# Expert batches of 4, 5 and 7 groups in units of 128 rows, and combining placed by a count of gathers, in a graph and mixture-of-experts kernel

## The reference, cut to what matters

```python
# x: (8192, 128), adj: (8192, 8192), 16 experts, 2 chosen for each row
msg = layernorm(x) @ W + B
weights = where(adj < 1, exp(-(1/adj - 1)**2 / 0.5), 0)
x = x + weights @ msg
z = layernorm(x)
logits = z @ gate_w + gate_b
vals, idx = top_k(logits, 2)
share = softmax(vals)
h = relu(z @ w1[e] + b1[e])                       # for each chosen expert e, 256 wide
moe = sum over the two of share * (h @ w2[e] + b2[e])
x = x + layernorm(z + moe) * gamma + beta
```

## Time and profile before

| | us |
|---|---|
| median of 3 runs | 1823.88 (1822.68 to 1824.42) |
| the profiled execution's span, first to last instruction | 1823.2 |
| PE busy | 1624.7 (89%) |
| ACT busy | 1565.7 (86%) |
| DVE busy | 1499.7 (82%) |
| POOL busy | 463.6 (25%) |
| chain of waits that ended last: PE L1118, PE L1137 | 48%, 24% of the span |
| mean granted clock of TensorE | 0.951 of 2.4 GHz |

### The profile page before, as it was taken

The page is one execution under the profiler, slowest core; times in us unless marked ns, Lnnn a source line. Parts: engine busy times, 40 slices in busy tenths (PEclk is TensorE's granted clock), DMA queues, the critical chain, the costliest instruction groups (busy, mean ns, idle before and its releaser), DMA issues.

```text
span 1823.2 us, 24195 instructions
## 1 busy us (share of the span) xinstructions
PE 1624.7 (89%) x8178; PEld 1073.6 (59%) x8178; DVE 1499.7 (82%) x2298; ACT 1565.7 (86%) x1502; POOL 463.6 (25%) x342
## 2 busy tenths in 40 slices
PE   4999999999999999999999999999999987384720
PEld 3666666666666666666666656666666786373620
DVE  7999998989899999999999989999998443153464
ACT  5899999999999999999999999999999664253531
POOL 0001223131314040407132231313140213535342
PEclk9999999999999999999999999999999999696765
DMA  9559867676767676776776676787673244343431
GB/s 313 158 160 290 235 199 215 195 217 193 214 195 212 196 212 198 220 213 202 210 202 209 199 210 199 209 247 208 202 206 121 80 124 143 87 141 97 129 110 50
DMA packets 216792, 338.22 MB, mean 186 GB/s; under 512 B 18080, under 2 KB 74144, under 8 KB 216544
## 3 DMA queue, kind: packets, MB, share of 16 engines
q1 hardware_dynamic: 208368, 319.62, 59.8%
q0 software_dynamic: 8304, 17.06, 3.1%
HBM read 303.07 MB, written 33.55 MB: 185 GB/s over the span
## 4 chain that ended last, share of the span: by engine, by line
PE 84%; DVE 6%; another core or an unknown queue 5%; issue 3%; ACT 1%; DMA 1%; DVEq 0%; SPq 0%; ACTq 0%
PE acc L1118 48%; PE tp L1137 24%; PE tp L1164 4%; PE tp L1192 3%; PE acc L1192 2%; DVE chunk L654 1%; PE tp L1153 1%; DVE stats L666 1%; DVE chunk L660 1%; DVE chunk L1004 1%; PE misc L1094 1%; ACT chunk L613 1%; DVE msg L729 1%; DMA xs<-in_x_dram 1%
## 5 line engine op out<-in xcount | busy, mean ns | idle before, releaser
L1118 PE MATMUL acc<-wT,msg 128*128 128x512 f32 x2048 | 976.0, 599 | 0.0
L527 ACT ACTIVATE wT<-tp 128x1024 f32<-128x1024 f32 x512 | 761.0, 1674 | 14.0 <-PE tp L1137 12.4
L521 ACT ACTIVATE chunk<-chunk 128x2048 f32<-128x2048 f32 x256 | 655.3, 2560 | 0.1
L660 DVE SCALAR_TENSOR_TENSOR chunk<-chunk 128x2048 f32<-128x2048 f32 x256 | 584.8, 2284 | 54.7 <-ACT chunk L521 54.1
L1137 PEld LDWEIGHTS tp<-ident,chunk 128*128 128x128 f32 x4096 | 478.7, 141 | 223.2 <-issue 221.5
L654 DVE SCALAR_TENSOR_TENSOR chunk<-chunk 128x2048 f32<-128x2048 f32 x256 | 583.5, 2280 | 1.9 <-DMA chunk<-in_adj_dram 1.9
L1137 PE MATMUL tp<-ident,chunk 128*128 128x128 f32 x4096 | 534.3, 274 | 0.0
L516 ACT ACTIVATE chunk<-chunk 128x4096 f32<-128x4096 f32 x118 | 511.0, 4331 | 0.0
L1118 PEld LDWEIGHTS acc<-wT,msg 128*128 128x128 f32 x2048 | 349.1, 190 | 258.3 <-issue 245.8
L457 POOL TENSOR_TENSOR pool_carrier<-pool_carrier 1x1 f32<-1x1 f32 x32 | 43.7, 1365 | 951.5 <-DVE row_now L845 825.9
L476 POOL DMA_INDIRECT rows_in<-y,row_now x128 | 216.7, 1693 | 40.4 <-issue 40.4
(11 more groups left out here) (121 smaller groups left out, 794.7 us busy)
## 6 DMA issues: line engine op xcount, KB each, us to landing
chunk<-in_adj_dram SPq DMA_DIRECT2D x256, 1024.0 KB, 5.4
chunk<-rows_in SPq DMA_DIRECT2D x118, 64.0 KB
rows_out<-chunk SPq DMA_DIRECT2D x59, 128.0 KB
chunk<-rows_in SPq DMA_DIRECT2D x35, 128.0 KB
rows_out<-chunk SPq DMA_DIRECT2D x17, 256.0 KB
y_kept<-y SPq DMA_DIRECT2D x16, 256.0 KB, 6.1
chunk<-y_kept SPq DMA_DIRECT2D x16, 256.0 KB
out_dram<-chunk SPq DMA_DIRECT2D x16, 256.0 KB
```

The lines of the kernel that those rows point to most:

```text
L521: act.activation(slot(c), slot(c), ACT.Exp, scale=-1.0).then_inc(inverted, 1)
L527: act.activation(wT[:, (g * PPG + m) % WSLOTS, :], tp[(g * PPG + m) % TSLOTS][:, :], ACT.Exp, scale=-2.0).then_inc(weighted, 1)
L660: dve.scalar_tensor_tensor(out=slot(c), in0=slot(c), scalar=2.0, in1=slot(c), op0=ALU.subtract, op1=ALU.mult).then_inc(squared, 1)
L1118: ins = pe.matmul(acc[:, :], msg[:, n, :], wT[:, (g * PPG + m) % WSLOTS, k * ROWS:(k + 1) * ROWS], start=(n == 0), stop=(n == 2 * PPG - 1))
```

## The change

BATCHES becomes (4, 5, 7) and TILES (1, 1, 1): 47, 55 and 71 units, all of 128 rows, 173 in all. The list `starts` is worked out from a count of gathers, in blocks of 128 rows: a batch's gathers begin 2 blocks after its last unit or when the group before is through, each of the eight takes 5/3 of a block, and a combine is placed where 4 blocks have passed after its group's last gather begins, or 11 places after the combine before. A combine that would stand behind the last unit is placed right behind it. The starts become 65, 78, 92, 105, 120, 133, 147, 160, 173, then 184 to 250 in steps of 11, and LAST becomes 263. GpSimd's program is left as it is, as are the places of the table and the zero rows. Beside this, the tables and zero rows of the first two batches move with FIRST to groups 5 and 10 of the adjacency stage (from 8 and 13).

```diff
-    BATCHES = (7, 5, 4)
-    TILES = (1, 2, 1)
+    BATCHES = (4, 5, 7)
+    TILES = (1, 1, 1)
...
-        COMBINE_WAIT, COMBINE_PACE, COMBINE_LONG = 8, 6, 11
-        starts = []
+        COMBINE_PACE, COMBINE_LONG = 6, 11
+        ROW_PACE, LANDED, GATHERED = 5 / 3, 2, 4
+        tiles_to = [0]
+        for u in range(NU):
+            tiles_to.append(tiles_to[-1] + TILES[batch_of(u)])
+
+        def units_at(t):
+
+            return next((u for u in range(NU + 1) if tiles_to[u] >= t), NU + math.ceil(t - tiles_to[NU]))
+
+        starts, free_at = [], 0
         for b, n in enumerate(BATCHES):
             for _ in range(n):
-                at = UNIT0[b + 1] + COMBINE_WAIT
-                pace = COMBINE_PACE if starts and UR[batch_of(starts[-1])] > P else COMBINE_LONG
-                starts.append(max(at, starts[-1] + pace) if starts else at)
+                at = [max(free_at, tiles_to[UNIT0[b + 1]] + LANDED) + kb * ROW_PACE for kb in range(KB)]
+                free_at = at[-1] + ROW_PACE
+                ready = units_at(at[-1] + GATHERED)
+                if ready > NU:
+                    ready = NU + 1
+                pace = COMBINE_PACE if starts and starts[-1] < NU and UR[batch_of(starts[-1])] > P else COMBINE_LONG
+                starts.append(max(ready, starts[-1] + pace) if starts else ready)
         LAST = starts[-1] + COMBINE_LONG + 2
```

## The result

The changed kernel takes 1857.26 us (median of 4 runs, 1855.38 to 1858.30) against 1823.28 of the kernel before (4 runs): a ratio of 1.018 with a 95% interval of 1.017 to 1.020. It is slower, by 34 us where the forecast had 7, and lies above the range of 1812 to 1848. The profiled execution took 1856.5 us and its span is 1854.8 us.

The account below looks back on a forecast made before the run. The prediction took GpSimd's back-to-back gathers, 1.25 us apart, to hold up signals beside units. Adjacency 1434.5, units 294.5 and tail 101 summed to 1830 us, 7 over the span before; range 1812 to 1848.

Parts of the forecast that it names:

- The tail, 101 us forecast: After the last unit: seven groups of gathers, disturbed combines and the last store, taken as 101 us, bounds 87 and 110.
- the mean rate of 0.64: Tail: combining goes at 0.64 of its undisturbed rate over the whole gather burst, giving a tail of 98 us.
- The text's other reading: Tail: one slow stretch at 0.36 of the rate from 36 us after the last unit, giving 106 us.
- bound of 110: Tail's upper bound: combining slow at 0.36 from 22.5 us into the burst on, 110 us.
- The first rival: Tail: combining keeps up with the gathers, so the tail is 87 us and the time 1816 us; chance 0.27.
- The units, 294.5 us forecast: Expert stage: 173 units between the adjacency work and the tail take 294.5 us, 18 us less than before.
- the bound of 1737: Expert stage: the units end at 1729 us, between 1719 and 1737.
- Fewer blocks, 15 us off: Expert stage: 173 blocks of 128 rows in place of 188, at 1.0 us each, save 15 us.
- Placing combining later wins and costs nothing: Expert stage: later combines neither gain nor cost time, since no combine waited for its gathers before.
- The joined stretch is worse than its parts: Both joined gather stretches and the tail cost 8 us more each as the lag grows: about 1852 us; chance 0.13.
- The third rival: Expert stage: something other than gathers caused the stalls, so units take 199 us, tail 87, total 1721 us; chance 0.05.
- the 87 us that the prediction worked out: Undisturbed tail: 75.5 us until the last gather lands, 8.4 for a combine and 2.8 for the last store.

Follow-up runs that it names:

- the spaced: The changed kernel with each gather beside units waiting for VectorE's unit count, 5/3 of a unit apart, tail gathers back to back: 1774.80 us, ratio 0.973.
- the plain kernel: The changed kernel with each of its 128 gathers by index replaced by a plain DMA of consecutive rows from GpSimd: 1722.99 us, ratio 0.941.
- the two sets without: Sets without held-up signals; the changed kernel with a 384-column memset before each tail gather alone took 1752.65 and 1754.88 us there, ratios 1.029 and 1.030.

## Why the prediction was wrong

*The direction and the order of events were right, the size was not:* 7 us over the kernel before were forecast and 32 came, by the spans. The bursts are of 4, 4, 1 and 7 groups and begin where the text put them: 1501.3 us, 1612.5, 1676.0, and 3.7 us after the last unit. The units nearly stop inside, and the cause named (gathers by index 1.25 us apart hold up signals) is shown by the spaced and by the plain kernel in their sets. The prediction spared the scatters; the last group's, back to back, do the same. Nearly all sizes were too small.

*The tail, 101 us forecast, 114.8 measured.* This is the step that failed, 14 of the 25 us by which the sum was short. The text took the mean rate of 0.64 over a burst of 41 us for one of 71. The rate isn't a mean: for 27 us after the burst begins signals come on time (the first late step is at 1771), and from then on two combines take 29.4 and 20.5 us, 0.28 and 0.41 of the undisturbed rate, the second with its last steps behind the burst. The longer a burst, the more of it is at the slow rate, and this one was 71 us. The text's other reading, one slow stretch, was right in shape and gave 106; even its bound of 110 was short, because 0.36 was read from a burst of four groups and the slow rate falls as the burst goes on. Another 1.0 us is in the first gather, 3.7 us after the last unit in place of 2.7. The first rival (combining keeps up until 55 us into the burst) is decided by the same rows: it begins at 27.

*The units, 294.5 us forecast, 305.0 measured.* Unit 60 stood at 1549.5 for 1546. Units 60 to 102 took 59.5 us for 53.5: combining and the table were priced at 11.5 us over 42 and cost 17.5; with plain DMAs, where nothing is held up, the same units still took 57.2, so most of that is their own work on busy engines. The second burst gave 52.5 us for 48.5, and the last stretch 78.5 for 81. The end at 1740.0 lies over the bound of 1737. These are the other 10 us.

*"Fewer blocks, 15 us off".* The run with 128-row units alone gained nothing. Between bursts the blocks are worth about 1 us each, but with fewer of them nothing of the bursts goes away.

*"Placing combining later wins and costs nothing".* It won nothing in the kernel before (1823.48 us), nor, as far as these runs tell, with the new batches.

*The rivals.* "The joined stretch is worse than its parts" gave "about 1852", the nearest number (its own terms, three times 8 us over 1830, make 1854), by a lag that grows within a burst. That growth is seen (15.47 us against 13.21, and the tail's rate), though the first joined stretch cost 3.5 us more than forecast, not 8; nearly all of the growth fell into the tail, where the text had it also. It had a chance of 0.13, too low: the range should have reached to it.

*The third rival*, a chance of 0.05, put the units at 199 us. Under hold-ups it is wrong by 106 us. In the two sets without, the same gathers beside the same units gave 210 and 213 us. What the prediction's argument could not see from one profile is that the hold-up is a condition of a set. The Trainium skill ("SBUF — State Buffer", "Who interferes with whom") has it that a DMA never contends with a compute engine. That rule is about the ports of the SBUF, and the prediction stretched it when it drew from it that gathers cost the units nothing: what comes late here is signals, and 2 units in 40.3 us with hold-ups against 27 in 42.8 without say nothing against the rule on ports.

*What stays open.* Why a set has the hold-ups; through what path signals are delayed; and the changed kernel's ratio without them. An estimate for that: last unit 1643.4 (measured with the same gathers), and the 87 us that the prediction worked out for an undisturbed tail, make 1730 us against 1704, slower by 1.6%. The tail of 105.2 us measured there, less 55 gaps between gathers that were some 0.3 us longer, gives 89 and bears the 87 out. The whole was not measured.

## What to carry to other kernels

Where the engines wait for each other every microsecond and GpSimd has many indirect DMAs to issue, put them one by one among its waits on the units' progress, and not back to back behind one wait. Here gathers 5/3 of a unit apart took 82 us off 1857. In the tail, 1.57 us apart took off some 10 and 1.4 us apart some 18, across sets. Beside units 4/3 of a unit was 13 us worse than 5/3. The price of such a burst isn't linear, so don't carry a mean rate from a short burst to a longer one. And compare the kernel before across sets before trusting a gain: the changed kernel spaced beside its units and at 1.4 us in its tail is 3.8% faster than the kernel before where signals are held up (1760.62 against 1829.91 us) and 2.4% slower where they aren't (1746.54 against 1703.72), so its gain is robustness more than speed. The old batches with spacing were not run in a set without hold-ups.

## What was not expected of the hardware

- The same kernel took 1703.7 us in one set and 1829.9 in the next, on the same chip, with medians of seven runs each that scatter by 0.1 to 0.3%, and with gathers issued at the same 1.25 us in both.
- Indirect DMAs at 1.25 us delay signals by up to 23 us in one condition; spaced at 1.57 us, in the tail, they delay none that can be seen; plain DMAs by the same engine at 0.53 us delay none that can be seen, in an execution in which scatters by index did. Where signals are held up, even two dependent steps of VectorE alone start 1.24 us late.
- A burst begins harmlessly in the tail (27 us without a delay) but at once beside the units, where unit signals are denser. That the density of signals is the reason is a guess.
